# An attention layer in float32 on one core: rounds written out, a two-engine start, and output products of the last batch by pairs

## What is computed

```python
scale_shift = emb @ W_emb + b_emb
scale, shift = jnp.split(scale_shift, 2, axis=-1)
xn = _rms_norm(x, g_norm) * (1.0 + scale) + shift
qkv = xn @ W_qkv                      # 1024 -> 3 x 16 heads x 64
q = _rms_norm(q, g_q)
k = _rms_norm(k, g_k)
logits = jnp.einsum('bhqd,bhkd->bhqk', q, k) * d ** (-0.5)
attn = jax.nn.softmax(logits, axis=-1)
o = jnp.einsum('bhqk,bhkd->bhqd', attn, v)
return o + o @ W_out                  # and the caller adds x
```

## Time and profile before

| | |
|---|---|
| Median of three runs | 2308.91 us (2307.57 to 2310.68) |
| The profiled execution's own time | 2310.12 us |
| Its span, first to last instruction | 2308.3 us |
| Mean granted TensorE clock | 0.993 |
| PE busy | 2272.3 us, 98% |
| DVE, ACT, POOL busy | 69%, 58%, 28% |

### The profile page before, as it was taken

How to read it: one execution, slowest core, us unless ns; L and a number is a source line. 1 busy time by engine, 2 the same in 40 slices (tenths; PEclk the granted TensorE clock), 3 DMA queues, 4 the chain that set the end, 5 groups by cost and what they waited for, 6 DMA issues and landing times.

```text
span 2308.3 us, 41569 instructions
## 1 busy us (share of the span) xinstructions
PE 2272.3 (98%) x13392; PEld 2117.6 (92%) x13392; DVE 1590.4 (69%) x3267; ACT 1342.0 (58%) x3101; POOL 653.5 (28%) x884
## 2 busy tenths in 40 slices
PE   7999999999999999999999999999999999999998
PEld 3999989999999999999999999999999999999987
DVE  2698794687837888287873878648785587846782
ACT  3687773567626676166752667436673467725661
POOL 3544431324213241132312233022330324202320
PEclk9999999999999999999999999999999999999999
DMA  7744236423364333633236232472314633344322
GB/s 292 269 178 174 111 143 213 191 98 115 118 222 183 110 110 109 231 137 110 110 121 248 107 114 107 135 279 99 125 65 171 244 110 110 110 168 161 110 110 89
DMA packets 71302, 346.70 MB, mean 150 GB/s; under 512 B 7600, under 2 KB 43440, under 8 KB 47536
## 3 DMA queue, kind: packets, MB, share of 16 engines
q1 hardware_dynamic: 71088, 344.01, 40.7%
HBM read 293.65 MB, written 50.33 MB: 149 GB/s over the span
## 4 chain that ended last, share of the span: by engine, by line
PE 94%; DVE 2%; issue 2%; ACT 1%; DMA 1%; POOL 0%; POOLq 0%; SPq 0%; DVEq 0%; ACTq 0%
PE proj_bank L479 20%; PE proj_bank L481 20%; PE proj_bank L480 20%; PE flip_bank L536 9%; PE score_bank L528 5%; PE pv_bank L545 5%; PE pv_bank L546 5%; PE score_bank L529 5%; PE flip_bank L501 2%; PE flip_bank L511 1%; PE proj_bank L557 1%; DVE neg_max L761 1%; PE score_bank L557 1%; DMA out<-res 0%; DVE probs L767 0%
## 5 line engine op out<-in xcount | busy, mean ns | idle before, releaser
L479 PE MATMUL proj_bank<-w_split,xn_hi 128*128 128x384 f32 x2048 | 702.2, 343 | 7.6 <-issue 4.0
L481 PE MATMUL proj_bank<-w_split,xn_lo 128*128 128x384 f32 x2048 | 690.7, 337 | 0.0
L480 PE MATMUL proj_bank<-w_split,xn_hi 128*128 128x384 f32 x2048 | 689.8, 337 | 0.0
L645 ACT ACTIVATE probs<-score_bank,neg_max 128x512 f32<-128x512 f32 x512 | 350.3, 689 | 177.8 <-DVE neg_max L761 172.6
L479 PEld LDWEIGHTS proj_bank<-w_split,xn_hi 128*128 128x128 f32 x2048 | 387.1, 189 | 26.8 <-issue 5.6
L480 PEld LDWEIGHTS proj_bank<-w_split,xn_hi 128*128 128x128 f32 x2048 | 387.2, 189 | 15.0
L651 ACT CAST pt_hi<-flip_bank 128x512 fp32r<-128x512 f32 x512 | 288.1, 592 | 193.4 <-PE pv_bank L546 133.0
L771 DVE TENSOR_TENSOR pt_lo<-flip_bank,pt_hi 128x512 fp32r<-128x512 f32 x512 | 341.1, 685 | 68.1 <-ACT pt_hi L651 65.8
L481 PEld LDWEIGHTS proj_bank<-w_split,xn_lo 128*128 128x128 f32 x2048 | 386.5, 189 | 0.0
L761 DVE TENSOR_REDUCE neg_max<-score_bank 128x1 f32<-128x512 f32 x512 | 335.6, 683 | 25.5 <-PE score_bank L529 24.2
L767 DVE TENSOR_SCALAR probs<-probs,row_inv 128x512 f32<-128x512 f32 x512 | 277.1, 541 | 18.1
(11 more groups left out here) (71 smaller groups left out, 3108.2 us busy)
## 6 DMA issues: line engine op xcount, KB each, us to landing
w_split<-w_store SPq DMA_DIRECT2D x140, 1536.0 KB, 7.3
w_store<-w_split SPq DMA_DIRECT2D x20, 1536.0 KB, 10.6
x_tile<-in_x SPq DMA_DIRECT2D x32, 512.0 KB, 11.2
w_split<-w_store SPq DMA_DIRECT2D x14, 1024.0 KB, 5.0
w_raw<-in_w_qkv SPq DMA_DIRECT2D x16, 768.0 KB, 8.2
w_raw<-in_x SPq DMA_DIRECT2D x56, 192.0 KB, 6.6
out<-w_raw SPq DMA_DIRECT2D x56, 192.0 KB, 1.9
emb_stage<-in_w_emb SPq DMA_DIRECT2D x5, 1024.0 KB, 11.1
```

What stands on the lines that cost most here:

```text
L479: nc.tensor.matmul(dst, a_hi, w_hi, start=(kt == 0), stop=False)
L480: nc.tensor.matmul(dst, a_hi, w_lo, start=False, stop=False)
L481: mm = nc.tensor.matmul(dst, a_lo, w_hi, start=False, stop=(kt == KT - 1))
L645: nc.scalar.activation(probs[h][:, i, :], score_bank[n % 2][:, :], ACT.Exp, bias=neg_max[:, n:n + 1], accum_out=row_sum[:, n:n + 1]).then_ ...
```

## The change

Five edits:

1. The loop is gone: `batches` calls the tables in Python, so six copies of `BODY` stand one behind the other, with constants in all waits and addresses.
2. Start: the first tile's transposes (X0) stand ahead of those of the modulation (new step Z0). Each bank of the condition's product has its own signal. `mod_now` of batch 0 comes from two DVE operations (one more, on `b_col`, stands ahead of the wait), and the modulation of all batches (`save_mod`) is made behind DVE's X0.
3. Batch 0's x: DVE and ACT modulate their halves at once. ACT rounds both (new step Y), DVE makes the first half's low part, and POOL the second's. The first two quarters of C wait for the first half alone.
4. Batch 7's output products: `last_product` does quarters 0 to 2 of each tile as one sum, which the new DVE step K adds to x, and quarter 3 of all tiles comes at the very end as a sum of its own, which R adds. The third group's weights go to `w_last`, which lies in `xn_hi` and has its own loads. Twelve places hold x (`w_raw` 0 to 7, `first_res`, `y_half1`), and all its loads stand early in the SP table.
5. New orders in parts of all tables: the middle of `HEAD`, parts of `BODY`, and `TAIL` from pair 3 on.

```diff
-            with engine.Fori(0, (B - 2) // 2) as m:
+            for m in range((B - 2) // 2):
                 cycle(BODY, m, 1)
                 cycle(BODY, m, 2)
...
+            def last_product(job, oc, tt, piece):
+                at, g, n = buf(job), oc * TT + tt, OUT_COLS[oc][1]
+                dst = proj_bank[g % 2][:, 0:n]
+                if piece in (0, 3):
+                    pe.wait_ge(proj_drained, LAST_TILE + (piece // 3 * NOUT * TT + g - 1))
+                for kt in (2 * piece, 2 * piece + 1):
...
+                    nc.tensor.matmul(dst, a_hi, w_hi, start=(kt in (0, KT - 2)), stop=False)
+                    nc.tensor.matmul(dst, a_hi, w_lo, start=False, stop=False)
+                    mm = nc.tensor.matmul(dst, a_lo, w_hi, start=False, stop=(kt in (KT - 3, KT - 1)))
+                    if kt in (KT - 3, KT - 1):
+                        mm.then_inc(proj_done, 1)
+            def turn_mod():
+                for cc in range(2 * KT):
+                    if cc % 4 == 0:
+                        pe.wait_ge(mod_rows_ready, cc // 4 + 1)
...
                     elif kind == "C":
-                        if p % PAIRS == 0 and i == 0:
+                        if p == 0 and is_first(b):
+                            if i == 0:
+                                pe.wait_ge(x_lo_first, h + 1)
+                            elif i == 2:
+                                pe.wait_ge(xn_lo_done, 2 * h + 2)
+                        elif p % PAIRS == 0 and i == 0:
...
+                    elif kind == "Y":
+                        act.wait_ge(flip_free, flip_at(order, b, "X", n // 2, 0)[0] + 2)
+                        round_x(n % 2, n // 2)
...
+            nc.vector.tensor_scalar(b_col[:, 0:KT], b_col[:, 0:KT], 1.0, None, ALU.add).then_inc(mod_step, 1)
+            dve.wait_ge(mod_step, 2)
             dve.wait_ge(mod_turned, 1)
...
+            nc.vector.tensor_tensor(mod_now[:, :], mod_turned_rows[:, :, 0], b_col[:, :], ALU.add).then_inc(mod_step, 1)
             dve.wait_ge(mod_step, 3)
...
+            nc.vector.tensor_tensor(mod_now[:, 0:KT], mod_now[:, 0:KT], g_col[:, :], ALU.mult).then_inc(mod_now_done, 1)
...
+                    elif kind == "Y":
+                        dve.wait_ge(xn_hi_done, 2 * n + 1)
+                        nc.vector.tensor_tensor(xn_lo[:, 0:4, n * P:(n + 1) * P],
+                                                y_half[0][:, :].rearrange("p (k t) -> p k t", k=4),
+                                                f32(xn_hi[:, 0:4, n * P:(n + 1) * P]), ALU.subtract).then_inc(x_lo_first, 1)
...
-                        dve.wait_ge(proj_done, count(out_job(m, c + d, oc)) * TT + (tt + 1))
                         res, at, uses = res_tile(b + d, n)
+                        if not is_last(b + d):
+                            dve.wait_ge(proj_done, count(out_job(m, c + d, oc)) * TT + (tt + 1))
+                        elif kind == "K":
+                            dve.wait_ge(proj_done, LAST_TILE + (n + 1))
+                        else:
+                            dve.wait_ge(proj_done, LAST_TILE + (NOUT * TT + n + 1))
+                            dve.wait_ge(proj_drained, LAST_TILE + (n + 1))
...
+            def load_last(half):
+                sp.wait_ge(proj_done, LAST_TILE)
+                n = OUT_COLS[NOUT - 1][1]
+                sp.dma_start(f32(w_last)[:, halves(half), :, :].rearrange("p k c n -> p (k c n)"),
+                             w_store[SLOTS - 1, :, half_of(half, n)]).then_inc(w_last_loaded[half], 16)
```

More of the change, by code:

```diff
@@ L229, in flip_buf, with releases @@
     return (before + places[0][(kind, n, p)][0]) % 2
+FIRST_X = {HEAD_FLIPS[0][("X", r, 0)][0] for r in range(TT)}
+def releases(order, u):
+    return u if order is HEAD and u - 2 in FIRST_X else u - 1
 def is_first(b):
-    return isinstance(b, int) and b == 0
+    return b == 0
 def is_last(b):
-    return isinstance(b, int) and b == B - 1
+    return b == B - 1
 def pair_job(m, c, p):
@@ L248, in out_job @@
 def out_job(m, c, oc):
-    last = isinstance(m, int) and 2 * m + c == B - 1
-    return m, JOBS * c + PAIRS + (0 if last else LATE) + oc
+    return m, JOBS * c + PAIRS + (0 if is_last(2 * m + c) else LATE) + oc
 def count(job):
@@ L381, in cond_attention @@
         w_loaded = [[sem(f"w_loaded{i}_{half}") for half in range(2)] for i in range(2)]
+        w_last_loaded = [sem(f"w_last_loaded{half}") for half in range(2)]
         w_used = sem("w_used")
@@ L496, in cycle @@
                     if kind == "T":
-                        wait_past(pe, flip_free, u - 1)
+                        wait_past(pe, flip_free, releases(order, u))
                         if n == 0:
@@ L505, in cycle @@
                         for half in range(2):
-                            wait_past(pe, flip_free, u + (half - 1))
+                            wait_past(pe, flip_free, releases(order, u + half))
                             if half == 0:
@@ L521, in cycle @@
                             pe.wait_ge(o_lo_done, b * PAIRS + (2 * piece + 2 + 1))
-                        product(out_job(m, c, oc), PAIRS + oc, tt, piece, o_hi, o_lo)
+                        if is_last(b):
+                            last_product(out_job(m, c, oc), oc, tt, piece)
+                        else:
+                            product(out_job(m, c, oc), PAIRS + oc, tt, piece, o_hi, o_lo)
+                    elif kind == "Z":
+                        turn_mod()
                     elif kind == "S":
@@ L976, in cycle @@
                     elif kind == "W":
-                        load_split(job, slot, half)
+                        if p is None and is_last(m * 2 + c + d) and slot == SLOTS - 1:
+                            load_last(half)
+                        else:
+                            load_split(job, slot, half)
                     elif kind == "X":
```

334 lines of the change are left out of this document (187 added, 147 removed).

## The result

| | before | after |
|---|---|---|
| median of its executions | 2308.24 us (four, 2305.51 to 2310.68) | 2279.21 us (four, 2277.75 to 2279.59) |
| ratio | | 0.9871, 95% interval 0.986 to 0.9883 |
| profiled execution, and its span | 2310.12, 2308.3 us | 2278.89, 2276.0 us |
| mean granted clock | 0.993 | 0.999 |

What follows compares the result with a forecast made beforehand. PE was taken as the bound, busy 2272.3 of 2308.3 us. Gains 7.5 + 4.7 + 1.0 + 3.5 + 12.7 + 1.0 = 30.4 off 2310.1 gave 2279.7, less 1.2 for the median: 2278.5, range 2270 to 2289.

Steps and rivals of the forecast that it cites:

- The loop, −7.5: Two backward jumps: writing the loop out removes 2.05 us idle and 3.42 us of half clock each, 7.5 us.
- The rival of straight code with stalls of its own: Six straight bodies: PE waits for instructions, 3.76 us each time; gain gone from 8 stalls on; chance 0.04.
- The start, −4.7: Before the first projection: shorter copy and modulation chain starts it at 41.2 instead of 45.94 us, gaining 4.7.
- The clock and the rest of x, −4.5 together: Batch 0: 1.0 us from less half clock behind the start, 3.5 us from later x tiles coming sooner.
- the case that I took: Clock behind the start: one 3.4 us half-clock stretch beginning near 40.5, projections paying 1.35 us; taken as −1.0.
- the middle of `HEAD`, which I had put at 0: New order in batch 0's middle: no gain counted, since only 1.9 us were idle in all.
- The last batch, −12.7: Batch 7: more P steps among the attention and quarter 3 last recover 13.7 us lost, less 1.0 for new waits.
- the 1.0 that I had put aside for new waits: Batch 7: allowance of 1.0 us for new waits and perhaps 0.3 of stores at the end.
- the 13.7 "lost now": Batch 7 before the change: idle time plus half of the half-clock busy time, 13.7 us from the windows view.
- The rival that K on DVE would stop PE: Batch 7: K queues among DVE's attention operations, PE waits at seven tiles, 7 us come back, 2285.5; chance 0.11.
- The rival of late weights: Batch 7: P16 waits for the second group's weights, about 5 us, 2283.5; chance 0.06.
- The orders, −1.0: `BODY` orders: 0.4 us exponential wait in each of six, at best 2.4 gone, at worst new ones; taken as −1.0.

Runs made afterwards that it cites:

- Experiment 6: Changed kernel, but ACT starts modulating its half of a batch 0 tile only when DVE has modulated the other half; 2278.44 us, ratio 0.9867.
- experiment 5: Changed kernel with 18 more PE transposes, results unread, behind the turns of the modulation at the start; 2280.07 us, ratio 0.988.
- experiment 7: Changed kernel with batch 0's x loads for the last two output tiles sent to free buffers and issued earlier, behind E8; 2276.92 us, ratio 0.986.
- experiment 8: Changed kernel with the edits of Experiment 4, experiment 5 and experiment 7 together, and steps `1L2` and `L3` moved later; 2272.19 us, ratio 0.984.
- experiment 2: Changed kernel with the last batch's lists, output products, loads and stores as before; 2294.22 us, ratio 0.9941.
- experiment 1: Kernel before the change with only its loop written out; 2301.3 us, ratio 0.9974.
- experiment 3: Changed kernel, split kept, but 15 of the 21 P steps among the last batch's attention moved behind `7W7`, K2 to K11 behind `7O1`; 2291.15 us, ratio 0.9921.
- Experiment 4: Changed kernel with the first part of each `BODY` list, up to pair 4, in the old order on PE, ACT, DVE and POOL; 2274.1 us, ratio 0.9854.

## Why the prediction was right, by its own steps

**The loop, −7.5: right.** The kernel with this edit alone gains 7.4 us in the six bodies (6.5 by the medians of the whole kernel), and nothing stands where the jumps stood. The rival of straight code with stalls of its own is refuted: batches 1 to 7, straight, show none. The Trainium skill ("Runtime: NRT & Kernel Launch", Instruction fetch mechanics) has sequential code fetched ahead with its cost mostly hidden; the trace agrees, with 278.3 to 278.5 us for each body.

**The start, −4.7: right in size, measured −4.4, with one step wrong.** Both halves side by side and DVE's low part came as worked out (0.69 us for the latter, 0.75 taken). I had let four of the sixteen turns stand behind the last copy, and ended them at 37.5. But the turns stand behind the first tile's transposes (35.83 to 36.85), the copies were done by 36.51, 0.7 earlier than forecast, and all sixteen turns ran after that, to 38.00. That they wait in four groups made no difference, and DVE's first modulation started at 38.52, not 38.1. Experiment 6 puts 1.5 us of the gain on the two engines working at once, in its one profiled execution.

**The clock and the rest of x, −4.5 together: right in sum, −4.3, the parts not shown.** The projections paid one short stretch (41.52 to 44.12 at half clock) instead of 4.85 us and a second stretch at 61. That is the case that I took. The other side of the weighing was the Trainium skill ("TensorE: Matmul & The Clock Gate", Part 1), which has activity release the throttled clock. I had read that as a release as long after the first projection as before, with nothing gained here. The trace disagrees with that reading, since PE's transposes from 40.14 on lie inside the stretch and it ended 2.60 us after the first projection, not 4.85. Experiments 5 and 6 moved the stretch both ways (none with PE kept busy, 6.8 us with a longer pause). By the windows the start's clock gained 4.85/2 − 2.60/2 = 1.1 and x gained 2.3 + 1.7 − 0.37 = 3.6 (44.12 to 64 us has 0.37 idle). The two cannot be told apart, and that the clock's part is worth 1.1 is not shown by a run: without the half clock (experiment 5) batch 0 took 1.2 us longer, with 3.4 us more of it (experiment 6) as long as now. What the clock gives there is in part waited for at the next tile of x. Against them stands the middle of `HEAD`, which I had put at 0: from 64 us to the end of batch 0 the waits of PE were 2.3 us before and are 3.5 after, of them 1.5 ahead of L553, up to 298.7 us, where none of that size was. Each row carries the error of busy sums that the paragraph on the last batch tells of, so they add up to 4.3 only roughly. The wait at 385 us (0.8 after, 0.7 before) is for a late load: with the load earlier (experiment 7) it is gone. With `L3` moved (experiment 8) the waits there are 0.2 and 0.7.

**The last batch, −12.7: right in mechanism, too small; measured −15.9.** The view shows no wait of PE there at all, so the 1.0 that I had put aside for new waits did not come. The rest, 2.2 us, is in the 13.7 "lost now" itself: I took it as length minus busy time, and a matmul record is longer than the time until the next one (0.28 us against 0.12 from start to start for 256 columns), so each of PE's pauses looks shorter than it is. Ten pauses of 0.20 us and more stand in the trace there; at 0.16 us each that is 1.6 of the 2.2, an estimate. That this makes the 2.2 is argued from these records, not shown by a run. And the 15.9 is that of one execution: the old orders of this batch took 232.6 us in before, 232.2 in experiment 2 and 231.4 in experiment 1, so the gain is 14.6 to 15.9. My bound of −13.7 fell with it. The rival that K on DVE would stop PE is refuted: DVE is busy for 27.32 us of the 44.00 in the attention, with PE never waiting. The rival of late weights too. What I had put down to the wait for `o_lo` (3.4 us, with half clock around it) is not a gain of its own: by experiment 3, removing that wait without the fill gave 1.6 us, with the new orders in it, and the fill, which the split makes possible, 13.9.

**The orders, −1.0: wrong, measured 0.** The wait for the exponential (0.4 us) went in each body, as I had expected it might, but one for `pt_lo` ahead of `3W2` came, of 0.6. Experiment 4 shows both at once: with the old first part and the new second part a body is 0.6 us shorter. I had looked for waits that the new order could remove and not costed those it could make.

**Against the time itself.** The spans differ by 32.3 us, the profiled executions by 31.2, the medians by 29.0. 1.1 of that lies outside the span (1.8 us before, 2.9 after; the other executions of after have 2.0 to 2.8), and 2.2 are the choice of execution: before's profiled one was 1.9 above its median, after's 0.3 below. So part of the closeness of 0.7 us is luck. Within the sum, 3.2 too little for the last batch stand against 1.0 too much for the orders and 0.5 for the start and batch 0. Outside it, the sum of 30.4 was 1.9 too small for the span, 1.1 of this went into the time outside it, and the median of after did not lie 1.2 below its profiled execution, as I had taken it from before, but 0.3 above. Why the time outside the span grew is open. It isn't the straight code as such: with the loop alone written out (experiment 1) it is 1.8 to 2.1 us in ten executions, and in experiments 5 and 8 1.7 to 1.9.

## What to carry to other kernels

Where one engine is the bound, its idle places are worth their length plus the half clock that follows them; independent matmuls put between dependent steps gained 13.9 us here, where removing the largest single wait of the same stage without them gained 1.6 at most. Splitting a sum where its late operand enters is what made these matmuls available early. A reordered list must be costed in both directions: look for the wait that it makes as well as for the one that it removes, and try its parts apart, since the best kernel here had the old order in one part and the new in the other. And time gained ahead of a producer that is just in time comes back as a wait (experiment 5), so such an edit is tried together with one that makes the producer earlier.

## What the runs showed of the hardware

- Half clock came in stretches of 3.41, 6.8 and 10.24 us in these kernels, after PE had been pausing, and went on through some busy microseconds behind. In the kernel with the loop written out alone, 10.24 us stood at the start (40.46 to 50.70); after has 3.41 there (40.70 to 44.12); eighteen transposes in the pause removed it (experiment 5), and in experiment 8 none is left up to the last matmul.
- A turn's end in the chip's loop cost PE 2.05 us of standing still and 3.4 us of half clock behind it, once in two batches; straight code of the whole program cost nothing that the trace shows.
- The ends of matmul records overlap the next ones. The changed kernel's timeline at the end of batch 0, with 256 columns each:

```profile
382.90 0.28 PE L501 MATMUL proj_bank<-w_split,o_hi 128*128 128x256 f32 x1
383.02 0.28 PE L502 MATMUL proj_bank<-w_split,o_lo 128*128 128x256 f32 x1
```

Distances between starts are the better ruler: busy sums hide a little of every pause.
